# The quotient of a decoder layer reads its reciprocals from SBUF in place of a copy in PSUM

## What is computed

```
q[t]   = d * q[t-1] + e[t]              (weights of the past)
p[t]   = d * p[t-1] + e[t] * v[t]       (weighted values of the past)
den[t] = bonus * e[t] + q[t-1]
num[t] = bonus * e[t] * v[t] + p[t-1]
y[t]   = num[t] / den[t]
```

## Time and profile before

| what | value |
|---|---|
| three runs | 411.26, 409.6, 411.18 us, median 411.18 |
| the profiled execution: its own time, its span | 412.55 us, 410.1 us |
| mean granted TensorE clock | 0.981 of full |
| PE busy | 370.8 us (90%) |
| DVE busy | 353.6 us (86%) |
| ACT busy | 318.7 us (78%) |
| POOL busy | 219.3 us (53%) |

### The profile page before, as it was taken

One profiled execution on the slowest core, in us unless ns is written; L12 is line 12 of the kernel. 1 busy time (PEld: TensorE's weight loads), 2 busy tenths in 40 slices (PEclk: granted clock), 3 DMA queues, 4 the chain that ended last, 5 costly groups with the idle time before them and its releaser, 6 DMA issues.

```text
span 410.1 us, 7960 instructions
## 1 busy us (share of the span) xinstructions
PE 370.8 (90%) x2774; PEld 289.9 (71%) x2774; DVE 353.6 (86%) x639; ACT 318.7 (78%) x420; POOL 219.3 (53%) x281
## 2 busy tenths in 40 slices
PE   7699899889997899999999999999999999659992
PEld 7698799768964788669775977497749785335541
DVE  3879898888788988988899988998899889898895
ACT  3677599769848989599959996799769994974782
POOL 1546772753355725674377535673566356644561
PEclk9989999999999999999999999999999999959999
DMA  7977456011110013000500050004000300000002
GB/s 257 361 273 269 164 195 243 2 53 27 59 46 0 2 48 134 0 28 2 179 2 27 2 179 2 26 0 154 25 0 26 129 0 0 26 2 18 36 26 77
DMA packets 12842, 31.74 MB, mean 77 GB/s; under 512 B 2038, under 2 KB 5132, under 8 KB 12812
## 3 DMA queue, kind: packets, MB, share of 16 engines
q1 hardware_dynamic: 12812, 31.35, 21.9%
HBM read 27.14 MB, written 4.21 MB: 76 GB/s over the span
## 4 chain that ended last, share of the span: by engine, by line
ACT 25%; PE 24%; issue 15%; DVE 14%; POOL 10%; POOLq 0%; ACTq 0%; DVEq 0%
PE proj_ps L530 13%; PE slot_ps L639 8%; POOL ring L1352 4%; ACT L1056 3%; ACT hqT L1021 2%; ACT ring L1014 2%; ACT L1060 2%; DVE inp L1545 2%; DVE x_max L1670 2%; ACT gate L897 2%; POOL gate L1292 2%; ACT q_state L962 2%; ACT q_state L956 2%; ACT gate L935 1%; ACT xqT L998 1%
## 5 line engine op out<-in xcount | busy, mean ns | idle before, releaser
L639 PE MATMUL slot_ps<-w1q,xqT 128*128 128x512 bf16 (+1 forms) x384 | 83.1, 367 | 5.1 <-DVE ring L1702 2.9
L1352 POOL TENSOR_TENSOR ring<-ring 128x512 f32<-128x512 f32 (+1 forms) x48 | 59.6, 1248 | 42.3 <-ACT ring L1007 41.1
L639 PEld LDWEIGHTS slot_ps<-w1q,xqT 128*128 128x128 bf16 x384 | 36.0, 99 | 44.7 <-issue 4.4
L530 PE MATMUL proj_ps<-x_high,proj_high 128*128 128x256 f32 x384 | 65.3, 292 | 1.7 <-DVE inp L1567 1.0
L530 PE MATMUL proj_ps<-x_high,proj_low 128*128 128x256 f32 x384 | 62.2, 284 | 0.0
L530 PE MATMUL proj_ps<-x_low,proj_high 128*128 128x256 f32 x384 | 62.0, 283 | 0.0
L530 PEld LDWEIGHTS proj_ps<-x_high,proj_high 128*128 128x128 f32 x384 | 53.6, 190 | 3.8 <-issue 1.6
L530 PEld LDWEIGHTS proj_ps<-x_high,proj_low 128*128 128x128 f32 x384 | 53.5, 191 | 0.0
L530 PEld LDWEIGHTS proj_ps<-x_low,proj_high 128*128 128x128 f32 x384 | 53.0, 189 | 0.0
L1327 POOL TENSOR_TENSOR den<-den,q_state 128x512 f32<-128x512 f32 x16 | 21.2, 1328 | 49.3 <-ACT q_state L962 48.9
L1007 ACT ACTIVATE ring<-ring,zero_bias,x_scale 128x512 f32<-128x512 f32 (+1 forms) x48 | 37.0, 775 | 9.5 <-DVE ring L1699 9.4
(11 more groups left out here) (157 smaller groups left out, 835.5 us busy)
## 6 DMA issues: line engine op xcount, KB each, us to landing
ring<-w_gate_up_dram SPq DMA_DIRECT2D x11, 512.0 KB, 4.2
forget<-xT_dram SPq DMA_DIRECT2D x8, 512.0 KB, 3.4
x_sb<-x_dram SPq DMA_DIRECT2D x8, 512.0 KB, 3.8
c_sb<-cT_dram SPq DMA_DIRECT2D x8, 512.0 KB, 4.5
out_dram<-late SPq DMA_DIRECT2D x12, 256.0 KB, 2.1
late<-w_down_dram SPq DMA_DIRECT2D x2, 704.0 KB, 6.9
ring<-w_down_dram SPq DMA_DIRECT2D x2, 704.0 KB, 4.2
scale_rows<-scratch_dram SPq DMA_DIRECT2D x2, 704.0 KB, 6.0
```

The costliest lines, as they stand in the source:

```text
L530: last = nc.tensor.matmul(out, a, b, start=(i == 0), stop=(i == len(terms) - 1))
L639: last = nc.tensor.matmul(slot_ps[:, s, half * 512:half * 512 + width], xqT[:, par, d, t * P:(t + 1) * P], w1q[:, d, half * I + at:half * ...
L1352: nc.gpsimd.tensor_tensor(hid, hid, gate_buf[:, at:at + width], ALU.mult).then_inc(hid_ready, 1)
```

## The change

`divide` multiplies `num` by the reciprocals where ACT wrote them, in `rec_copy` in SBUF, and waits for the semaphore of `reciprocal`. `place_reciprocal` and its semaphore are gone, at all eight places (16 instructions). The product still goes to `turn_feat` in PSUM.

```
-            def place_reciprocal(b, h):
-
-                act.wait_ge(rec_copy_ready, 2 * b + h + 1)
-                act.wait_ge(num_ready, 2 * b + h + 1)
-                nc.scalar.activation(blocks(turn_feat, h), blocks(rec_copy, h), ACT.Identity,
-                                     bias=zero_bias[:, :]).then_inc(rec_ready, 1)
...
                 reciprocal(b + 1, 0)
-                place_reciprocal(b + 1, 0)
                 reciprocal(b + 1, 1)
-                place_reciprocal(b + 1, 1)
                 round_hidden(n, 0, 0)
...
             def divide(b, h):
 
-                dve.wait_ge(rec_ready, 2 * b + h + 1)
+                dve.wait_ge(rec_copy_ready, 2 * b + h + 1)
                 dve.wait_ge(num_ready, 2 * b + h + 1)
                 nc.vector.tensor_tensor(blocks(turn_feat, h)[:, :, 1:], blocks(num, h)[:, :, 1:],
-                                        blocks(turn_feat, h)[:, :, 1:],
+                                        blocks(rec_copy, h)[:, :, 1:],
                                         ALU.mult).then_inc(y0_ready, 1)
```

More of the change, by code:

```diff
@@ L335, in decoder_layer @@
         rec_copy_ready = sem("rec_copy_ready")
-        rec_ready = sem("rec_ready")
         newton_ready = sem("newton_ready")
@@ L1158, in _ @@
             reciprocal(0, 1)
-            place_reciprocal(0, 0)
-            place_reciprocal(0, 1)
             silu_tables()
@@ L1191, in _ @@
             reciprocal(1, 1)
-            place_reciprocal(1, 0)
-            place_reciprocal(1, 1)
             silu_tables()
@@ L1235, in _ @@
             silu(6, 0, 1, [0])
-            place_reciprocal(7, 0)
-            place_reciprocal(7, 1)
             round_hidden(12, 0, 0)
```

## The result

The changed kernel takes 416.37 us (median of 6 runs, 414.95 to 420.34), the kernel before, run beside it, 410.93 (6 runs, 409.46 to 413.56): a ratio of 1.0141, with a 95% interval of 1.0090 to 1.0191. (The ratio is estimated from all runs of both kernels and need not be the quotient of the medians.) That is slower, by 5.4 us, where the prediction's sum had 3.7. The profiled execution took 414.95 us with a span of 412.4; the one of before took 412.55 with a span of 410.1.

The account below looks back on a forecast made before the run. PE was taken to bound the kernel, busy 41.67 of 42.65 us a pass. Passes 2.5, batch 1 0.95 and batch 0 0.25 summed to +3.7 us on the 411.18 median: 414.9 us, range 408.8 to 418.5.

Parts of the forecast that it names:

- the prediction's sum: Whole kernel: 2.5 us in five passes, 0.95 at batch 1, 0.25 at batch 0, zero at batch 7; +3.7 us.
- The direction and the mechanism: Slower: DVE's two-SBUF-input divides and POOL's SBUF products take turns by whole instructions, in order of asking; chance 0.50.
- I count no difference: Divide's own length: 689 ns with an input in PSUM, 687 for a like product from two SBUF tensors.
- The passes: Five passes: divides leave DVE 1.48 us late with 0.92 to spare, gating 0.5 later; +2.5 us in all.
- The gain of 0.45 us: Five passes, without anything else: ACT's second gate read starts 0.09 us earlier per pass, then PE is late.
- POOL comes ahead of gating in all or some passes: Rival: POOL's hidden goes first and holds DVE; 1.8 us a pass, +10.2 in all, 421.4 us; chance 0.12.
- Batch 1: Prologue: divides and Newton products take turns, gating starts at about 114.05 against 113.07; +0.95 us.
- batch 0: Prologue: Newton products and divides take turns, two refine end at 71.65 against 71.40 for gating; +0.25 us.
- `turn_values` would come up to 1.4 later: Batch 1: upper end of the delay; with 1.4 there and 0.56 a pass the sum is +4.5.
- The tail: Batch 7: second divide held back 0.3 us, covered, so zero; 0.3 us at most if the cover were gone.
- the cover of 0.69 us: Batch 7: refine ends at 370.33 and turn_values starts at 371.02, covering a second divide 0.3 us late.
- how much slack the engine that gets the new wait had (0.92 us against 1.48): Passes: DVE idles 0.92 us before gating, while the turns make it 1.48 us late; gating 0.5 later.

Follow-up runs that it names:

- e2_num_in_psum: Changed kernel with the numerator written to PSUM, so divide has one PSUM and one SBUF input; 410.24 us, ratio 0.9974.
- e6_residual_later: Changed kernel with POOL's residual_3 moved behind the next hidden product and DVE's layer_norm_3 behind layer_norm_2; 427.42 us, ratio 1.0397.
- e1_operand_only: Kernel before with only divide's operand changed to rec_copy in SBUF, copies and their semaphore kept; 415.84 us, ratio 1.0102.
- e4_copies_gone: Changed kernel whose divide reads turn_feat in PSUM again, where no reciprocals are put, so the result lacks the quotient; 410.52 us, ratio 0.9976.
- e3_interleaved: Changed kernel with DVE order divide, refine, divide, refine in the passes and batches 0 and 1; 412.18 us, ratio 1.0027.
- e10_psum_gating_first: e2_num_in_psum plus one prologue wait on POOL, so hidden of tile 0 follows gating of batch 2; 408.65 us, ratio 0.9947.
- e9_busy_and_gating_first: Changed kernel with 28 more dummy PE transposes before turn_values of batch 1, and POOL waiting for gating in the passes; 415.45 us, ratio 1.0096.

## Why the prediction was right, and where it fell short

*The direction and the mechanism* were right. The first divide was to end 0.54 us after `newton`, then `residual_3` to take its turn and end 1.14 later, then the second divide: the trace has 0.56, 1.14 and 0.56. The operand alone makes the loss, and with one input in PSUM or the divides apart it goes. The Trainium skill (SBUF — State Buffer, Who interferes with whom) says that a DVE instruction with two SBUF inputs and a GpSimd one that reads SBUF lock each other out as wholes; the trace agrees, and adds who is next.

*The size of a divide.* "I count no difference" held: a divide with one input in SBUF and one in PSUM takes 687 ns in the middle, before the change and in e2_num_in_psum, and an unblocked one from SBUF alone 684 to 690 (e6_residual_later, and the first of batch 7 in the changed kernel). By the estimate from the Trainium skill (VectorE: DVE Perf Modes, the TRN2 errata) the latter would be 65 ns shorter; no run shows that, and the measurement decides.

*The passes.* 0.5 us each was forecast. Four of the five lost 0.32, 0.65, 0.45 and 0.35, on average 0.44. The third lost 1.41. With the copies still in place (e1_operand_only) the five lose 0.43 to 0.53. The gain of 0.45 us that the missing copies were to bring in the passes is 0.8 in e4_copies_gone.

*What fell short* is how the rival "POOL comes ahead of gating in all or some passes" was used. The prediction saw that only 0.1 to 0.2 us kept the two in order, gave the rival 0.12, and let its range hold two or three such passes. But it priced the bad order for all five passes only, and put none of it into the sum; a single pass had no term. It was the third, in all four profiles with this order (the three of the changed kernel and the one with PE kept busy), at 1.4 us over the kernel before, where the rival had 1.8 for each pass.

The runs show where the slack went. `hidden` is issued 0.23, 0.20, -0.08, 0.21 and 0.14 us behind the start of `gating` in the five passes of the changed kernel. In its second pass one read by ACT comes late against PE. Here are ACT and PE:

```profile
233.07 0.69 ACT L896 ACTIVATE inp<-proj_ps,zero_bias 128x512 f32<-128x512 f32 x1 [0.74 <-PE proj_ps L529]
```

```profile
232.03 0.64 PE L529 MATMUL proj_ps<-x_low,proj_high 128*128 128x256 f32 x4
```

PE ends at 232.67, the read starts 0.40 later, where 0.12 is usual; in the fourth pass it is 0.20. That is 0.28 and 0.08 late, and the order in the passes that follow has 0.28 and 0.07 less to spare than in the passes just before them. In e3_interleaved, where the order holds, the third pass has 0.38 us between the two and its neighbours 0.66. The equal sizes speak for this read as the reason; no run was made to test it. It doesn't come from the turns: the read in the second pass starts 0.40 behind PE in all kernels without the copies, also in those whose divides never wait (e2_num_in_psum, e4_copies_gone, e10_psum_gating_first), and 0.12 in the two with them, the kernel before and e1_operand_only. Why the missing copies delay it stays open.

*Batch 1* lost 0.92 us against 0.95, batch 0 0.30 against 0.25. But "`turn_values` would come up to 1.4 later" was used only as an upper end of delay. It came 1.4 later (7.51 us after the batch's logarithm instead of 6.13), and what wasn't priced is that PE stands idle for it: in one of three profiles of the changed kernel the granted clock behind it was 0.54 to 0.61 and 1.5 us more went.

*The tail* was put at zero and gave back 0.34, just what the fifth pass had lost: the cover of 0.69 us held for the second divide's 0.35, and it was itself a wait for PE, which is shorter now.

*The sum*, +3.7, stands against +4.06 in the first profile, +4.0 in the third and +5.6 in the second, and +5.4 in the medians. With the third pass's order and the wait at batch 1 taken away (e9_busy_and_gating_first) it is +3.7, in part by luck, as said there. The time, 416.37, is 1.5 us above the forecast of 414.9 and well inside the range. In the first and third profiles the sum is 0.3 to 0.4 us too low: the third pass's 0.9 over its forecast, less what the tail gave back and small differences. The rest, 1.4 us between the first profile's +4.06 and the medians, is not in these two traces, and what it is was not shown. The granted clock is a candidate: the two longest of the six runs, 417.72 and 420.34, have the lowest mean clock, 0.979, against 0.981 to 0.984 in the others.

## What to carry to other kernels

On DVE, an operand's place is no matter of cycles here (684 to 690 ns either way) but of company: beside a POOL that works in SBUF, keep one input of each DVE product in PSUM, or at least put work with a PSUM input between two products that have none. Ask of a removed step how far behind the next engine is (PE was 0.1 us behind ACT in the passes, so 1.4 us of ACT's queue a pass bought 0.8 in all five) and how much slack the engine that gets the new wait had (0.92 us against 1.48). Where two instructions are in order by one or two tenths of a microsecond, expect both orders, and either write the order down or price the bad one for some of the passes.

## What the hardware did that I had not expected

- A kept order among waiters makes the second of two products much dearer than the first: 0.95 us, then 1.78, with `residual_3` asked in between; 0.95 and 1.06 with a `refine` between them; 0.68 with nothing queued on POOL. Writing to PSUM doesn't exempt a product with two SBUF inputs: all these divides write there.
- The same 1.99 us wait of PE was followed by a granted clock of 1.00 in two profiles of the changed kernel and of 0.54 and 0.61 in another, at 1.5 us. Over all kernels it was low in two of seven such profiles. What decides it stays open.
- The wait for `gating` on POOL cost 0.15 to 0.18 us in three passes where it changed no order, so a written order isn't free.
- Taking two copies out of ACT's queue made one of its reads, some 35 us later, start 0.40 us behind PE in place of 0.12: in the second pass, in all twelve profiles of kernels without the copies.
